# Value products of the last 26 keys: the second group of four heads on swapped column halves

## The reference, cut to what matters

```
q = (queries @ Wq + bq).reshape(b, nq, 16, 64)
k = (keys @ Wk + bk).reshape(b, nk, 16, 64)
v = (values @ Wv + bv).reshape(b, nk, 16, 64)       # nk = 154
att = einsum(q, k) / 8 * attention_weights
att = softmax(where(attention_mask, -inf, att))
out = einsum('bhqk,bhkd->bhqd', att, v).reshape(b, nq, 16 * 64)
return out @ Wo + bo
```

## Time and profile before

| what | value |
|---|---|
| median of three runs | 640.88 us |
| lowest, highest run | 638.73, 641.42 us |
| the profiled execution, device time | 641.74 us |
| its span, first to last instruction | 639.9 us |
| TensorE busy | 593.4 us, 93% of the span |
| weight loads busy | 452.6 us |
| VectorE, ScalarE, GpSimd busy | 433.4, 315.1, 237.3 us |
| mean granted TensorE clock | 0.974 of full speed |

### The profile page before, as it was taken

One profiled execution on the slowest core, in us unless ns is written; L12 is line 12 of the kernel. 1 busy time (PEld: TensorE's weight loads), 2 busy tenths in 40 slices (PEclk: granted clock), 3 DMA queues, 4 the chain that ended last, 5 costly groups with the idle time before them and its releaser, 6 DMA issues.

```text
span 639.9 us, 11015 instructions
## 1 busy us (share of the span) xinstructions
PE 593.4 (93%) x3621; PEld 452.6 (71%) x3621; DVE 433.4 (68%) x802; ACT 315.1 (49%) x992; POOL 237.3 (37%) x227
## 2 busy tenths in 40 slices
PE   5989999898999998999999979999999999999990
PEld 3446647786878787687787858687777777777770
DVE  2899999789786869548686496633576555555550
ACT  4532343298787972958929567414322222222220
POOL 2011010236545536536246474331235333333332
PEclk9999999999999997999999996997999999999996
DMA  9900002547142304304125049572434433443325
GB/s 308 364 2 2 1 1 79 198 140 276 50 177 80 120 2 138 127 12 188 34 82 176 10 144 300 165 284 64 116 91 82 68 60 60 66 68 64 53 34 156
DMA packets 36648, 70.98 MB, mean 111 GB/s; under 512 B 5185, under 2 KB 29473, under 8 KB 34081
## 3 DMA queue, kind: packets, MB, share of 16 engines
q1 hardware_dynamic: 28272, 59.16, 27.9%
q0 software_dynamic: 7152, 9.34, 8.7%
q10 hardware_dynamic: 1168, 1.78, 0.8%
HBM read 58.83 MB, written 17.48 MB: 119 GB/s over the span
## 4 chain that ended last, share of the span: by engine, by line
PE 54%; DVE 13%; ACT 9%; issue 9%; DMA 9%; POOL 3%; POOLq 1%; ACTq 0%; DVEq 0%; SPq 0%
PE pb L546 8%; PE pb L454 7%; DMA zs_dram<-R 7%; PE pb L657 6%; PE pb L568 6%; PE pb L471 4%; PE pb L397 3%; PE pb L578 3%; PE pb L677 3%; ACT R L773 3%; DVE R L971 3%; PE pb L513 2%; ACT R L785 2%; PE pb L497 2%; PE pb L440 2%
## 5 line engine op out<-in xcount | busy, mean ns | idle before, releaser
L773 ACT ACTIVATE R<-R,mx 128x154 f32<-128x154 f32 x256 | 104.5, 425 | 0.0
L657 PE MATMUL pb<-R 128*128 x312 | 98.8, 460 | 0.3 <-ACT R L879 0.3
L1477 POOL DMA_INDIRECT zs_dram<-R x39 | 60.5, 1552 | 100.7 <-DVE R L1343 59.1
L883 ACT ACTIVATE R<-R 128x352 f32<-128x352 f32 x39 | 19.4, 497 | 115.8 <-DVE R L1333 115.8
L657 PEld LDWEIGHTS pb<-R 128*128 128x128 f32 x312 | 56.2, 190 | 25.4 <-issue 0.8
L454 PE MATMUL pb<-xnT,wq 128*128 128x256 f32 x256 | 58.4, 384 | 3.3 <-DVE R L1039 2.5
L766 ACT ACTIVATE R<-pb,bq 128x256 f32<-128x256 f32 x64 | 30.0, 474 | 63.0 <-PE pb L454 63.0
L677 PE MATMUL pb<-R 128*128 (+1 forms) x234 | 57.0, 380 | 0.0
L546 PE MATMUL pb<-wo,R 128*128 128x256 f32 x256 | 56.8, 380 | 0.0
L454 PEld LDWEIGHTS pb<-xnT,wq 128*128 128x128 f32 x256 | 47.9, 191 | 11.9 <-DVE R L1039 3.5
L546 PEld LDWEIGHTS pb<-wo,R 128*128 128x128 f32 x256 | 48.5, 190 | 7.4 <-issue 0.8
(11 more groups left out here) (153 smaller groups left out, 1122.8 us busy)
## 6 DMA issues: line engine op xcount, KB each, us to landing
R<-in_fside_dram SPq DMA_DIRECT2D x16, 1232.0 KB, 5.6
R<-in_L_ffn_w_dram SPq DMA_DIRECT2D x16, 352.0 KB, 4.7
R<-xs_dram SPq DMA_DIRECT2D x39, 129.0 KB, 2.1
R<-in_mask_dram SPq DMA_DIRECT2D x16, 308.0 KB, 2.9
KV<-in_ebias_dram SPq DMA_DIRECT2D x2, 1440.0 KB, 10.5
zs_dram<-x SPq DMA_DIRECT2D x4, 512.0 KB, 3.1
R<-in_L_ffn_w_dram SPq DMA_DIRECT2D x8, 256.0 KB, 4.4
zs_dram<-in_x_dram SPq DMA_DIRECT2D x1, 1920.0 KB, 9.1
```

Source lines behind the costliest of these rows:

```text
L657: ins = e.matmul(pb[:, u.i, 0:F], xsT[:, s % 2, k, :], ew13[:, bass.ds(w_reg[s] * 1408 + q * 704 + k * F, F)], start=(k == 0), stop=(k == 1))
L773: ins = e.activation(att[t % 3][:, h, :], att[t % 3][:, h, :], ACT.Exp, bias=mx[:, a4, 1, h:h + 1], accum_out=mx[:, a4, 2, h:h + 1])
L1477: e.indirect_dma_start(out=zs, out_offset=bass.IndirectOffsetOnAxis(ap=xsl[:, s % NR, D:D + 1].bitcast(U32), axis=0), in_=sY[:, s % 4, :], ...
```

## The change

The second four heads of each half (`g = 1`) change places in pairs: their head with an even number goes to the second column half, the one with an odd number to the first. The eight small matmuls are then issued as row groups 0, 2, 1, 3 of `g = 0`, followed by 0, 2, 1, 3 of `g = 1`, and use eight different pairs of row group and column half. The four increments of `full` stay four; they are now on row groups 1 and 3 of each `g`, which are the last writers of the two banks of that `g`. In the eight large matmuls of L513 the column halves become 0, 1, 0, 1, 1, 0, 1, 0. The bias `bvT` and the rows of `Wo` are laid out on the host in an order, `CROSSED`, that undoes the swap; `Wv` keeps `ORDER`. Number, shape and operands of all instructions stay, no wait is added or removed.

```
+CROSSED = [ORDER[i ^ (i // 4 % 2)] for i in range(H)]
@@ product, TensorE
                 for n in range(8):
-                    u, to = uses[n // 2], 64 * (n % 2)
+                    u, to = uses[n // 2], 64 * (n % 2 ^ n // 4)
                     w.wait_ge(free[u.e], u.empty)
                     e.matmul(pb[to:to + 64, u.i, 0:256], vm[b][:, 8 * hf + n, :], turned_in(n), start=True, stop=False)
-                for turn in range(2):
-                    for i, r in enumerate((0, 2, 1, 3)):
-                        g = i // 2 ^ turn
-                        u, to = uses[2 * g + r // 2], 64 * (r % 2)
+                for g in range(2):
+                    for r in (0, 2, 1, 3):
+                        u, to = uses[2 * g + r // 2], 64 * (r % 2 ^ g)
                         ins = e.matmul(pb[to:to + 64, u.i, 0:256], vr[b][32 * r:32 * r + 32, 2 * hf + g, :],
                                        turned_in(8 + g)[32 * r:32 * r + 32, :], start=False, stop=True)
-                        if turn:
+                        if r % 2:
                             ins.then_inc(full[u.i], 1)
@@ host
-    o["bvT"] = np.ascontiguousarray(a["L0_xattn_bv"].reshape(H, 64)[ORDER].reshape(8, P).T)
-    o["L0_xattn_Wo"] = np.ascontiguousarray(a["L0_xattn_Wo"].reshape(H, 64, D)[ORDER]).reshape(1024, D)
+    o["bvT"] = np.ascontiguousarray(a["L0_xattn_bv"].reshape(H, 64)[CROSSED].reshape(8, P).T)
+    o["L0_xattn_Wo"] = np.ascontiguousarray(a["L0_xattn_Wo"].reshape(H, 64, D)[CROSSED]).reshape(1024, D)
```

## The result

The changed kernel took 632.23 us (median of four executions, 631.63 to 633.90) against 639.89 us for the kernel before (four executions): a ratio of 0.9883, with a 95% interval of 0.9851 to 0.9915. That is 7.7 us where 3.3 were forecast, and outside the range that was given. Executions more than 1.5% above the fastest one of the same kernel are left out of the comparisons, one in e2 and six of the kernel before; with those six the mean gain of the three further measurements would be 3.2 instead of 2.9 us. So there are two questions: whether the forecast mechanism is there, and what the rest of the first number was.

The account below looks back on a forecast made before the run. TensorE was taken as the bound only between waits for other engines. Units 0 to 2 (0.6 + 0.6 + 0), units 3 to 7 (2.0) and clock (0.1) gave 3.3 us off 640.88: 637.6 us, range 635.0 to 641.8.

Parts of the forecast that it names:

- Two bunches instead of four, s = 0.40: Small matmuls (L518): eight different tiles start in two bunches instead of four, saving 0.40 us per product, 6.4 us of TensorE.
- The lower end of the bound: Small matmuls (L518): eight tiles gain nothing, since four at once is all that any row shows.
- the rivals of three or four bunches: L518: engine doesn't look far enough ahead; three bunches give 639.3 us, four 640.9 us; chance 0.17 together.
- The large matmuls, 0: Large matmuls (L513): the turned order of column halves costs 0; upper end 0.21 us per product, 1.7 us on the path.
- Unit 0, 0.6: Unit 0: both products save 0.80 us, but `combined` waits for VectorE's L1078 and gives 0.2 back, leaving 0.6.
- Unit 1, 0.6: Unit 1: 0.2 us of the first product's saving counts because of ScalarE's copy, the second product's counts whole; sum 0.6.
- Unit 2, 0: Unit 2: ScalarE runs on without a pause and TensorE then waits for VectorE, so nothing is saved.
- the wait of 2.83 us: TensorE's wait for VectorE at 242.83, forecast to grow by 0.4 to 0.8 us as a sign of being right.
- Units 3 to 7, 5 x 0.40: Units 3 to 7: first products' savings end in a stall, second products' 0.40 us each count; sum 2.0 us.
- The clock, plus 0.1: Unit 6, where the clock halved inside L518: up to 0.7 us could be saved, 0.1 was added.
- a rival with extra falls: Longer idles in units 3 and 4 halve the clock: two new falls 644.4 us, one 641.0; chance 0.10.
- A run's spread of 0.9 us: Whole kernel: a run's spread of 0.9 us, allowed around the no-gain time of 640.9 us in setting the range.

Follow-up runs that it names:

- e2: The kernel before as a run of its own, no edit: ratio 0.9995, nine executions, mean 639.9 us.
- three further measurements: The changed kernel run three more times without edit, 12 executions each, against the kernel before: ratios 0.9964, 0.9964 and 0.9961.
- after: The profiled execution of the changed kernel from the first measurement, whose median was 632.23 us against 639.89 us, ratio 0.9883.
- e3: Column halves crossed for heads 0 to 7 alone (each unit's first product), against the kernel before: 0.9998.
- e13: The changed kernel a fourth time, no edit, against the kernel before: 0.9961, mean 636.0 us.
- e1: The changed kernel once more, no edit, against the kernel before: 0.9964, mean 637.1 us.
- e5: The changed kernel a third time, no edit, against the kernel before: 0.9964, mean 635.2 us.
- before: The profiled execution of the kernel before the change: 641.74 us; the kernel's median in the first measurement was 639.89 us.
- e4: Column halves crossed for heads 8 to 15 alone (each unit's second product), against the kernel before: 0.9953.
- e9: The changed kernel with ScalarE's last two copies after four exponentials instead of six, against the kernel before: 0.9885.
- e12: The kernel before with ScalarE's last two copies after four exponentials instead of six, nothing else changed: 0.9930.
- e8: The kernel before with the new issue order on the old four tiles: 641.0 us in one execution.
- e14: The changed kernel with ScalarE's last two copies after four exponentials, repeated on another chip, against the kernel before: 0.9864, mean 630.0 us.
- e6: The kernel before with two extra matmuls on TensorE ahead of the last unit's product with Wo: 1.0027, mean 640.1 us.

## Why the prediction was wrong, by its steps

- **Two bunches instead of four, s = 0.40.** Right, to the hundredth: 0.69 instead of 1.09 us, eight records started within 0.05 us. The lower end of the bound (nothing) and the rivals of three or four bunches are out. Eight records start together, two for each row group. So the rule of the Trainium skill that was weighed against the change (TensorE: Matmul & The Clock Gate, Part 3, The mechanism: weight loads overlap only between different row groups) doesn't hold here: the weight loads of the fifth to the eighth tile start at 156.80 to 156.82 us, while the matmuls on the same four row groups, started at 156.78 to 156.80, run for 0.43 us.
- **The large matmuls, 0.** Right: 1.95 us.
- **Unit 0, 0.6.** It was 0.82. The 0.2 us of giving back didn't happen. In the trace of after the first of VectorE's two L1078 ended at 162.56, and the ninth record of `combined` started at 162.74, 1.83 us behind the first record, as before. Only its weight load came later, 1.70 instead of 1.62 us behind the first record. I had let TensorE need the data a whole record earlier; the later load delayed no matmul.
- **Unit 1, 0.6.** Measured 0.56, and e3 gives the first product 0.16, the expected 0.2.
- **Unit 2, 0.** Right for the path: unit 2 is 0.28 us shorter, and it is given back in unit 3. But not in the wait of 2.83 us, which I had said would grow by 0.4 to 0.8: it is 2.83 again. The gap is inside the 24 scores at the start of unit 3, which take 2.16 us from 234.10 instead of 1.89 from 236.39.
- **Units 3 to 7, 5 x 0.40.** Right where it can be read. Units 4, 5 and 7 show 0.41, 0.41 and 0.40; in units 3 and 6 the clock covers it. e3 shows 0.01 to 0.02 in units 4, 5 and 6 for the first products alone, and 1.48 for 1.08 us in the stalls of units 3 and 4 says where it went. In unit 6 I had the place wrong: the stall on ScalarE's copy stayed at 1.79 us, and the 0.40 went into TensorE's wait ahead of it (L353, 1.87 us for 1.46).
- **The clock, plus 0.1, and a rival with extra falls.** This is the step that failed. The direct sum came out at 3.4 us, but I treated the three stretches at half clock as given, put 0.1 us for them into the sum and allowed only for more of them. In the traces 23.9 us at half clock became 10.2, worth some 5 us. The range, down to 635.0, was built from direct costs and didn't contain that. The repeats show that this isn't a gain of the change: over 36 executions its mean clock was no higher. What the term lacked is scatter in both directions, of 5 us for 0.010 of mean clock, and the first measurement fell on its fast side, by luck as far as the runs tell. Two new falls at the stalls of units 3 and 4 didn't come either, at an idle of 1.48 us. That rival wanted an idle time that decides, between 1.08 and 1.79 us; the falls behind unit 7 came in e13 and not in after, with the same idles of 0.43 and 0.77 us ahead, so idle time alone doesn't place a fall.
- **A run's spread of 0.9 us.** Also too small. Three executions lay within 2.7 us; 69 of them range from 632 to 643 us, with a standard deviation of 2.6, of which 1.2 to 1.5 are left at equal clock. Medians of four then differ by chance by a few us.

What stays open is the first measurement itself. Its four executions had granted clocks of 0.983, 0.980, 0.980 and 0.980. Of the 36 later ones on three chips 12 had 0.980 or more. Four of four is rare by chance alone (about 1 in 80), so a property of that chip or of that moment isn't excluded; three chips didn't show it. Its mean, 632.5 us, is 3.6 us under that of the 36, of which the clock makes 1.9 by the line; its four executions of the kernel before, 640.0 in the mean, are 1.0 us over the 69. The 1.7 us that are left are about twice what a mean of four scatters by at equal clock, and stay without a cause. What is shown is that its 4.4 us over the forecast are not direct work saved.

## What to carry to other kernels

Give small matmuls that are issued near each other different pairs of row group and column half, and check it by how many records start within a few hundredths of a microsecond; the order of issue among them didn't matter here. A saving on the bounding engine counts only up to its next wait that ended with another engine's own work: go from stall to stall and give each saving to the stall that follows it, then look at what ends that stall, since moving that (two exponentials behind two copies) was worth 2.3 us beside the 3.3 of the change. Where the clock falls to half in the trace, each of these stretches is a term of the range in both directions, and a difference of a few microseconds between two single traces must be taken apart into direct steps and clock before it is believed.

## What the runs showed of the hardware that I had not expected

Eight 32 x 64 tiles run together with 0.02 us more delay than four: 0.47 us for the first bunch of eight against 0.45 us for four, and the second bunch ends 0.22 us later.

Executions of one program on one core differ by 2.5 us of standard deviation, and their times go with the mean granted clock, 5.0 us for 0.010; 1.5 us are left beside that line. The profiled executions are no fair sample of it. Those of the change had mean clocks of 0.976 to 0.983 (after, e1, e5, e13), those of the kernel before 0.974 and 0.974 (before, e2), a difference that the 36 and 69 executions don't show.

A second source of scatter is in unit 7. In e1 ScalarE's last two copies came about 2 us later than in the trace of after, with nothing of the program that would hold them. ScalarE's timeline of e1:

```profile
409.47 0.59 ACT L785 COPY R<-pb 128x512 f32<-128x512 f32 x1 [4.34 <-remote]
410.91 0.59 ACT L785 COPY R<-pb 128x512 f32<-128x512 f32 x1 [0.86 <-remote]
```

"remote" says that the profile shows nothing that released the instruction. The unit takes 24.2 to 24.3 us where this happens in the chip of e1 to e4. The same delay is in the traces of e9 to e12, from a second chip, and in none of the six from the two others (e5 to e8, e13, e14), where the unit takes 22.3 to 23.0 us (23.6 with the extra work of e6). So it goes with the chip as far as these traces tell. In e1, where the expert weights are fetched at that time, the DMA engines are busy for 0.98 of the time from 400 to 405 us and for 0.50 from 405 to 411.5. What ScalarE waits for there stays open.
